# A graph network on one core: a batch's message sums share one PSUM bank and one stored block

## The chip, the cores and the metric

The kernel runs on one core of a Trainium2 chip. The metric is the device time in microseconds (us) of one execution, the lower the better. The profile times every instruction of one execution; its rows name the engines PE (TensorE's matmuls), PEld (its weight loads), DVE (VectorE), ACT (ScalarE), POOL (GpSimd) and SP (SyncE, which here only issues transfers). A name that ends in q, as SPq or PEldq, is the engine's sequencer: register work, semaphore waits and the issue of transfers.

## The reference

50000 nodes with 128 features, 50000 edges (src, dst), sorted by dst. Two parts follow each other; the change is in the two layers of the second.

```
x = layernorm(x + graph_convolution(x, src, dst))
h = x @ W_enc.T + b_enc
for l in range(2):
    m = concatenate([h[src], h[dst]], axis=-1)
    m = relu(m @ msg_W1[l].T + msg_b1[l])
    m = m @ msg_W2[l].T + msg_b2[l]
    agg = segment_sum(m, dst)
    upd = concatenate([h, agg], axis=-1) @ upd_W[l].T + upd_b[l]
    h = layer_norm(h + upd)
out = layernorm(x + h @ W_out.T + b_out)
```

## The kernel before

The work is a row of stages with a barrier of all engines behind each: rank, place and plan (they sort the edges into tiles and make tables), edges, conv and nodes (the convolution), and then for each layer `edges0`/`edges1` (message stage: `edge_stage` with `degrees` false) and `nodes0`/`nodes1` (node stage: `node_stage`). The second node stage also makes the output ("final").

**Tiles and steps.** Edges are cut into 392 tiles of 128, nodes into 392 tiles of 128, four to a chunk of 512 nodes, 98 chunks. A list of 784 steps walks through both: step s belongs to one edge tile and one node tile, and advances either one. Four steps make a batch, so a message stage has 196 batches. As dst is denser at low numbers and the walk starts at the high ones, a batch of the first 49 takes 1.4 new edge tiles on the mean and one of the last 49 takes 2.9.

**A batch in the message stage.** GpSimd gathers the src rows of each edge tile from `table_p` with an indirect transfer into `ring` (64 tiles; L851), in groups of four, 392 gathers in all; before it reuses a place it waits for the batch that read it last (`tile_end`, `s_pq`). SyncE loads the dst side, `q_ring`, chunk by chunk. ScalarE makes a one-hot matrix `turned` (L965, L967). PE's `combine` adds, for each of the four steps, the gathered rows (a product with the identity, L1011) and the dst rows picked by `turned` (L1012) in `ps_m`. ScalarE takes the relu into `msg` (L979). PE's `segment` multiplies it with `onehot`, which VectorE makes in `hot` (L868), into four column blocks of `ps_a` (L1021), one for each step. PE's order is: segment of batch i-2, combine of batch i. VectorE's `chain` then adds each step's block into its node tile in `acc` (L883), a sum that is kept in SBUF for 8 chunks; each of the four waits for the one ahead (`s_chain`). A chunk that is complete is stored by SyncE as one block of `table_t` (L826), 98 stores for a layer, and the next `q_ring` chunk is then loaded (L828).

**The node stage.** For chunk c SyncE's `load` brings the sums (`in_a` from `table_t`, L1250) and the layer's input (`in_z`, L1256), each 256 KB; PE's `update` (L1381, L1382), `flip_z` and `project` take 20 matmuls for a chunk; `store` of chunk c-7 puts `table_z` and `table_p` away (L1269, L1271). In the final stage SyncE brings `in_z` of the first layer again (L1261) and stores the output of chunk c-11 (L1266). The order on SyncE is fixed, in a hardware loop over four chunks at a time:

```
pipelined(sp, [(load, 0)] + ([(load_x1, 4), (store, 11)] if final else [(store, 7)]))
```

`load` waits until PE has used the buffer of chunk c-4 (`s_sum`). The four input buffers let the loads run up to three chunks ahead.

Of the kernel before, what the change touches and what calls it, by code (L numbers as in the profile page):

```python
# [8 lines left out]
P = 128  # L9
N, E, D, L = 50000, 50000, 128, 2  # L10
J = 4
# [19 lines left out]
HR, QR, BEHIND = 3, 3, 2  # L31
XR = 4
# [51 lines left out]
def parts(c):  # L84

    return LAST if is_last(c) else P

# [428 lines left out]
def plan_stage(nc, m):  # L516

    K = TP // 4
    with ExitStack() as ctx:
# [16 lines left out]
        n_s, n_c, e_s, lo, hi, loc, ge, past, within = (sb(n, [P, S]) for n in ("n_s", "n_c", "e_s", "lo", "hi", "loc", "ge", "past", "within"))  # L536
        ti = sb("ti", [1, 9, S], I32)
        tf, ends = sb("tf", [1, 3, NCHUNK]), sb("ends", [1, 4, 3 * EW], I32)
# [10 lines left out]
        with nc.Block() as block:  # L549
# [20 lines left out]
            def _(dve):  # L570
# [53 lines left out]
                nc.vector.memset(ends[:], 1)  # L624
                link(nc.vector.tensor_copy(int_row[:, 0, :], m.incl[:, 0:TP]))
# [4 lines left out]
                dve.sem_inc(s_rows, 1)  # L630

# [31 lines left out]
                link(nc.vector.tensor_scalar(ge[:], lo[:], m.lane[:], None, ALU.is_le))  # L663
                link(nc.vector.tensor_tensor(within[:], ge[:], past[:], ALU.mult))
# [25 lines left out]
                pack(table[:, :, 1], 5, [of(8, 3)] + [of(3, j) for j in range(4)], 7)  # L690
                nc.vector.tensor_copy(m.slots[:, 0:NB], table[:, :, 1])
# [9 lines left out]
                for k, to in ((0, m.chunk_end), (3, m.tile_end)):  # L701
                    pack(to[:, 0:EW], 10, [ends[:, k, :].rearrange("o (w j) -> o w j", j=3)[:, :, j] for j in range(3)], 10)
# [61 lines left out]
def edge_stage(nc, m, table, table_q, agg, degrees, x=None):  # L764


    F = P + 1 if degrees else P
    AW = W if degrees else P
    AR = 3 if degrees else QR
    where = (lambda j: (j // 2) * 512 + (j % 2) * W) if degrees else (lambda j: j * P)  # L770
    with ExitStack() as ctx:
# [3 lines left out]
        ring, first = m.ring, PRE // 4 if degrees else 0  # L775
        q_ring = None if degrees else sb("q_ring", [P, RC * CH])
        acc = sb("acc", [P, 4 * RC * AW])
        onehot = sb("onehot", [P, HR, 4, P])
        if not degrees:
            turned, msg = sb("turned", [P, QR, CH]), sb("msg", [P, QR, CH])  # L780
            d_ring = sb("d_ring", [P, DR, DB * CH], F16)
            ps_m = pb("ps_m", 512, QR)
        else:
            xin, x_t, r_out = sb("xin", [P, XR, CH]), sb("x_t", [P, 2, CH]), sb("r_out", [P, XR, CH])
# [13 lines left out]
        with nc.Block() as block:  # L798
# [35 lines left out]
            def _(pool):  # L834
                if degrees:
                    pool.sem_inc(s_prow, first)
# [717 lines left out]
```

## Time and profile before

| | us |
|---|---|
| device time, median of 3 runs (3956.29 to 3964.6) | 3957.3 |
| the profiled execution: its span, first to last instruction | 3444.6 |
| median less that span (what lies around it) | 512.7 |
| message stage of layer 0, from its first gather to the next stage's first load | 544.5 |
| node stage of layer 0, from its first load to the next stage's first gather | 410.4 |
| final node stage, from its first load to the end of the span | 367.5 |

The page of the profile gives no own device time for the profiled execution beside its span. The span is made of stages one after another, so the sum of the stages' lengths is the span; whatever is saved or lost in a stage is saved or lost in the time, and what lies around the span stays.

### The profile page before, as it was taken

To read this page: it belongs to the slowest core of one execution; us is meant where nothing else is said; L and a number is where in the kernel's file an instruction comes from. 1 tells how busy PE (TensorE), PEld (TensorE's weight loads), DVE (VectorE), ACT (ScalarE), POOL (GpSimd) and SP (SyncE) were. 2 spreads that over 40 slices of the span, in tenths; PEclk is the share of its full clock that TensorE was granted. 3 is DMA by queue.
4 is the path that set the end of the run, shared out by engine and by line. 5 is a ranking of instruction groups with operands and counts; after the bars stand their busy time and mean duration, and the time that the engine had idled before them with its cause. 6 is when DMAs were issued, how large, how long until landed. Compare 5 with 4: busy or idle time off the path is not lost. (4 is left out here: it accounts for less than half of the span.)

```text
span 3444.6 us, 92529 instructions
## 1 busy us (share of the span) xinstructions
PE 2975.2 (86%) x25312; PEld 2674.1 (78%) x25312; DVE 2700.0 (78%) x8634; ACT 2379.7 (69%) x5642; POOL 1846.0 (54%) x1782
## 2 busy tenths in 40 slices
PE   4975656777767789997999998999979999989998
PEld 3753334555543378987999998999979999989998
DVE  9999967888856688885777776666657777769998
ACT  3779945777742368886777775666657777759999
POOL 0000036577755533335776776555547767766664
PEclk9999988999979989999999999999989999999999
DMA  0027635777649989997776654999977766548887
GB/s 21 2 69 229 223 103 162 221 219 215 195 139 340 346 280 355 366 356 250 225 221 208 191 158 123 327 327 326 328 239 229 221 210 194 164 129 287 296 295 240
DMA packets 460711, 777.79 MB, mean 226 GB/s; under 512 B 113689, under 2 KB 115865, under 8 KB 460393
## 3 DMA queue, kind: packets, MB, share of 16 engines
q1 hardware_dynamic: 355046, 548.85, 48.2%
q10 hardware_dynamic: 67714, 147.73, 12.5%
q0 software_dynamic: 37632, 77.15, 9.2%
q8 instruction: 178, 2.92, 0.3%
q14 instruction: 141, 1.15, 0.1%
HBM read 451.50 MB, written 321.78 MB: 224 GB/s over the span
## 5 line engine op out<-in xcount | busy, mean ns | idle before, releaser
L883 DVE SCALAR_TENSOR_TENSOR edges_acc<-edges_acc,keep,edges_ps_a 128x128 f32 (+1 forms) x2352 | 820.3, 349 | 272.1 <-issue 145.9
L851 POOL DMA_INDIRECT ring<-table_p,esrc x784 | 787.5, 1004 | 313.3 <-issue 206.0
L1011 PE MATMUL edges_ps_m<-ring,ident 128*128 x3136 | 609.7, 276 | 33.8 <-POOLq L840 33.8
L1012 PE MATMUL edges_ps_m<-edges_q_ring,edges_turned 128*128 x3136 | 608.8, 276 | 0.0
L1011 PEld LDWEIGHTS edges_ps_m<-ring,ident 128*128 128x128 f32 x3136 | 478.6, 193 | 34.7 <-ACT edges_turned L967 17.7
L1012 PEld LDWEIGHTS edges_ps_m<-edges_q_ring,edges_turned 128*128 128x128 f32 x3136 | 478.8, 193 | 0.0
L979 ACT ACTIVATE edges_msg<-edges_ps_m 128x512 f32<-128x512 f32 x392 | 234.2, 597 | 295.5 <-PE edges_ps_m L1012 294.7
L1021 PE MATMUL edges_ps_a<-edges_onehot,edges_msg 128*128 128x128 f32 x3136 | 414.0, 275 | 0.0
L851 POOL DMA_INDIRECT ring<-table_h,esrc x344 | 327.7, 953 | 138.5 <-issue 93.5
L1021 PEld LDWEIGHTS edges_ps_a<-edges_onehot,edges_msg 128*128 128x128 f32 x3136 | 381.7, 192 | 0.0
L868 DVE TENSOR_TENSOR edges_onehot<-iota,drel 128x512 f32<-128x512 f16 x441 | 305.0, 692 | 96.1 <-PE edges_ps_a L1021 94.0
L1286 POOL TENSOR_TENSOR nodes_extra<-ub,deg 128x512 f32<-128x512 f32 x196 | 203.8, 1040 | 285.8 <-DVE nodes_y L1443 244.9
L1036 PEld LDWEIGHTS edges_ps_a<-ring,edges_onehot 128*128 128x128 f32 x1568 | 195.5, 196 | 175.9 <-issue 104.1
L1381 PE MATMUL nodes_ps_y<-uw,nodes_in_a 128*128 128x128 f32 x1568 | 306.0, 277 | 19.4 <-DMA nodes_in_z<-table_z 19.4
L1382 PE MATMUL nodes_ps_y<-wproj,nodes_in_z 128*128 128x128 f32 x1568 | 305.5, 277 | 0.0
L1407 PE MATMUL nodes_ps_p<-wproj,nodes_z_t 128*128 128x128 f32 x1568 | 303.2, 275 | 0.0
L1406 PE MATMUL nodes_ps_q<-wproj,nodes_z_t 128*128 128x128 f32 x1568 | 303.1, 275 | 0.0
L1036 PE MATMUL edges_ps_a<-ring,edges_onehot 128*128 x1568 | 224.0, 287 | 90.8 <-DVE edges_acc L883 47.5
L965 ACT ACTIVATE edges_turned<-edges_d_ring,minus_lane 128x512 f32<-128x512 f16 x392 | 279.3, 712 | 21.8 <-DMA edges_d_ring<-table_d 21.6
L967 ACT ACTIVATE edges_turned<-edges_turned,one 128x512 f32<-128x512 f32 x392 | 283.1, 722 | 12.8
L1454 DVE BATCH_NORM_STATS2 nodes_st<-nodes_y 128x6 f32<-128x128 f32 x1176 | 255.6, 280 | 6.9
L1289 POOL TENSOR_TENSOR nodes_extra<-nodes_extra,bu 128x512 f32<-128x512 f32 x196 | 249.8, 1274 | 15.4
(315 smaller groups left out, 6776.2 us busy)
## 6 DMA issues: line engine op xcount, KB each, us to landing
table_z<-nodes_z_t SPq DMA_DIRECT2D x196, 256.0 KB, 5.0
table_p<-nodes_p_out SPq DMA_DIRECT2D x196, 256.0 KB
table_q<-nodes_q_out ACTq DMA_DIRECT2D x196, 256.0 KB
edges_q_ring<-table_q SPq DMA_DIRECT2D x196, 256.0 KB, 4.8
edges_d_ring<-table_d ACTq DMA_DIRECT2D x98, 512.0 KB
table_t<-edges_acc SPq DMA_DIRECT2D x196, 256.0 KB
nodes_in_a<-table_t SPq DMA_DIRECT2D x196, 256.0 KB
nodes_in_z<-table_z SPq DMA_DIRECT2D x196, 256.0 KB, 4.3
```

The costliest lines, as they stand in the source:

```text
L851: nc.gpsimd.indirect_dma_start(out=ring[:, e % RE * W:e % RE * W + P], out_offset=None, in_=table[:, :], in_offset=bass.IndirectOffsetOnAx ...
L868: nc.vector.tensor_tensor(onehot[:, i % HR, :, :], m.iota[:, 0:P].unsqueeze(1).to_broadcast([P, 4, P]), m.drel[:, 4 * i:4 * i + 4].unsquee ...
L883: nc.vector.scalar_tensor_tensor(out=to, in0=to, scalar=m.keep[:, s:s + 1], in1=ps_a[:, i % AR, where(j):where(j) + F], op0=ALU.mult, op1= ...
L967: nc.scalar.activation(to, to, ACT.Relu, bias=m.one[:], scale=-1.0).then_inc(s_turned, 1)
L1011: nc.tensor.matmul(to, m.ident[:], rows[j], start=True, stop=False)
L1012: last = nc.tensor.matmul(to, turned[:, i % QR, j * P:(j + 1) * P], slots[j], start=False, stop=True)
L1021: last = nc.tensor.matmul(ps_a[:, i % QR, j * P:(j + 1) * P], msg[:, i % QR, j * P:(j + 1) * P], onehot[:, i % HR, j, :], start=True, stop ...
L1036: last = nc.tensor.matmul(ps_a[:, i % AR, where(j):where(j) + F], onehot[:, i % HR, j, :], rows[j], start=True, stop=True)
L1381: nc.tensor.matmul(to, part(in_a, b, j), m.uw[:, layer, :], start=True, stop=False)
L1382: last = nc.tensor.matmul(to, part(in_z, b, j), m.wproj[:, layer, 2 * D:3 * D], start=False, stop=True)
L1406: nc.tensor.matmul(part(ps_q, b % 2, j), part(z_t, b, j), m.wproj[:, nxt, D:2 * D], start=True, stop=True)
L1407: last = nc.tensor.matmul(part(ps_p, b % 2, j), part(z_t, b, j), m.wproj[:, nxt, 0:D], start=True, stop=True)
```

## The change

**Message stage** (now `message_stage`; `edge_stage` keeps only the convolution). `combine` leaves the identity product out for steps 0 and 1 of a batch (`ADDED = 2`); VectorE's `add_rows` adds those two gathered rows to `ps_m` where it lies in PSUM. `segment` puts the four products of a batch into one PSUM bank at the place of the node tile, counted from the tile of step 0 (`m.wins` holds the distances), so that steps of one tile add up in PSUM. VectorE's `move` then takes the bank to SBUF, `window`: the first 128 columns with what the window before carried over for that tile, the other 384 by a copy. ScalarE stores every window as one block of `table_w` (`store`), 196 for a layer and 256 KB each. `q_ring` chunks wait for `combine` (`q_end`) and no longer for a finished sum.

**Node stage.** The sums of a node tile now lie in some block of `table_w`; `m.where` says in which one and at which of its four places. `load` reads four words of it and brings the four tiles of a chunk with four transfers of 64 KB.

**Plan stage.** It makes the tables `wins`, `carry`, `where` and `q_end`.

The diff, cut to its core:

```diff
+ADDED, WR, STORE = 2, 6, 4
...
-                def chain(i):
-                    dve.wait_ge(s_seg, i + 1)
-                    for j in range(4):
-                        s = 4 * i + j
-                        if s >= 1:
-                            dve.wait_ge(s_chain, s)
-                        nc.vector.scalar_tensor_tensor(out=to, in0=to, scalar=m.keep[:, s:s + 1], in1=ps_a[:, i % AR, where(j):where(j) + F],
-                                                       op0=ALU.mult, op1=ALU.add).then_inc(s_chain, 1)
+                def add_rows(i):
+                    rows = [ring[:, bass.ds(value(i, 1 + j), P)] for j in range(ADDED)]
+                    dve.wait_ge(s_pq, i + 1)
+                    for j in range(ADDED):
+                        last = nc.vector.tensor_tensor(tile(ps_m, i, j), tile(ps_m, i, j), rows[j], ALU.add)
+                    last.then_inc(s_add, 1)
+
+                def move(i):
+                    carried = window[:, (i - 1) % WR, bass.ds(value(i, 0) % J * P, P)]
+                    dve.wait_ge(s_seg, i + 1)
+                    if i >= 1:
+                        dve.wait_ge(s_win, 2 * i)
+                    if i >= WR:
+                        dve.wait_ge(s_out[i % WR], 16 * (i // WR))
+                    nc.vector.scalar_tensor_tensor(out=window[:, i % WR, 0:P], in0=carried, scalar=m.keep[:, 4 * i:4 * i + 1], in1=tile(ps_a, i, 0),
+                                                   op0=ALU.mult, op1=ALU.add).then_inc(s_win, 1)
+                    nc.vector.tensor_copy(window[:, i % WR, P:CH], ps_a[:, i % QR, P:CH]).then_inc(s_win, 1)
+
+                for i in range(NB + BEHIND):
+                    if i >= BEHIND:
+                        move(i - BEHIND)
+                    if i + 1 < NB:
+                        fetch(i + 1)
+                        hot(i + 1)
+                    if i < NB:
+                        add_rows(i)
...
+                def store(i):
+                    act.wait_ge(s_win, 2 * i + 2)
+                    act.dma_start(m.table_w[i * P:(i + 1) * P, :], window[:, i % WR, :]).then_inc(s_out[i % WR], 16)
...
                     for i in range(NB):
                         if i + 2 < NB:
                             turn(i + 2)
-                        act.wait_ge(s_pq, i + 1)
+                    if i >= STORE:
+                        store(i - STORE)
+                    act.wait_ge(s_add, i + 1)
...
-                    for j in range(4):
-                        nc.tensor.matmul(to, m.ident[:], rows[j], start=True, stop=False)
-                        last = nc.tensor.matmul(to, turned[:, i % QR, j * P:(j + 1) * P], slots[j], start=False, stop=True)
+                    for j in range(J):
+                        if j >= ADDED:
+                            nc.tensor.matmul(tile(ps_m, i, j), m.ident[:], rows[j], start=True, stop=False)
+                        last = nc.tensor.matmul(tile(ps_m, i, j), tile(turned, i, j), slots[j], start=j < ADDED, stop=True)
...
+                    if i % 4 == 0:
+                        spots[0] = loaded(nc, mybir.EngineType.PE, m.wins[0:1, i:i + 4])
+                    to = [tile(ps_a, i, 0)] + [ps_a[:, i % QR, bass.ds(spots[0][i % 4] // (1 << (2 * j - 2)) % J * P, P)] for j in range(1, J)]
+                    for j in range(J):
+                        last = nc.tensor.matmul(to[j], tile(msg, i, j), onehot[:, i % HR, j, :], start=j == 0, stop=True, skip_group_check=True)
...
                     else:
                         sp.dma_start(in_z[:, b, :], m.table_z[layer][bass.ds(c * P, P), :]).then_inc(s_z[b], 16)
+                        at = loaded(nc, mybir.EngineType.SP, m.where[0:1, bass.ds((NC - 1) * J - c * J, J)], S - 1)
+                        for j in range(J):
+                            sp.dma_start(in_a[:, b, j * P:(j + 1) * P],
+                                         m.table_w[bass.ds(at[j] // J * P, P), bass.ds(at[j] % J * P, P)]).then_inc(s_a[b], 16)
```

**SyncE in the node stage.** These are all of SyncE's instructions for one chunk inside the hardware loop of the layer 0 node stage, before the change; ISA is a group of register operations that sets an address.

```order
L1248 REGISTER_ALU
L1250 ISA
L1250 DMA nodes_in_a<-table_t 128x512
L1256 DMA nodes_in_z<-table_z 128x512
L1268 REGISTER_ALU
L1269 ISA
L1269 DMA table_z<-nodes_z_t 128x512
L1271 ISA
L1271 DMA table_p<-nodes_p_out 128x512
```

This is how the same chunk begins in the changed kernel; L92 is the helper that reads words of a table into registers.

```order
L1387 REGISTER_ALU
L1395 ISA
L1395 DMA nodes_in_z<-table_z 128x512
L92 REGISTER_ALU
L92 ISA
L92 TENSOR_LOAD where
L1398 ISA
L1398 REGISTER_ALU
L1398 DMA nodes_in_a<-table_w 128x128
```

The last three rows stand there four times; after them come the rows of `table_z` and `table_p` as before. A chunk's transfers on this queue go from four to seven, and a read of registers stands between the first and the second.

**PE in the message stage.** One batch before the change (segment of one batch, combine of another), where the names are those of the section on the kernel.

```order
L1021 MATMUL edges_ps_a<-edges_onehot,edges_msg 128x128 x4
L990 REGISTER_ALU x2
L1000 ISA x7
L1011 MATMUL edges_ps_m<-ring,ident 128x128
L1012 MATMUL edges_ps_m<-edges_q_ring,edges_turned 128x128
```

The last two rows stand there four times. After the change:

```order
L1193 ISA x3
L1201 MATMUL edges_ps_a<-edges_onehot,edges_msg 128x128 x4
L1174 REGISTER_ALU x2
L1178 ISA x5
L1185 MATMUL edges_ps_m<-edges_q_ring,edges_turned 128x128 x2
L1184 MATMUL edges_ps_m<-ring,ident 128x128
```

One more L1185, L1184 and L1185 follow. The matmuls of a batch go from 12 to 10 and the address groups from 7 to 8, three of which now stand ahead of the segment.

**VectorE in the message stage** had `hot`, four L876 ISA and four L883 for a batch. It now has this.

```order
L1103 ISA
L1109 SCALAR_TENSOR_TENSOR edges_window<-edges_window,keep,edges_ps_a 128x128
L1111 COPY edges_window<-edges_ps_a 128x384
L92 TENSOR_LOAD carry
L1089 TENSOR_TENSOR edges_onehot<-iota,drel 128x512
L1095 ISA
L1098 TENSOR_TENSOR edges_ps_m<-edges_ps_m,ring 128x128 x2
```

Three of four chained sums are gone; a copy of 384 columns, two additions and, every second batch, a read of registers have come.

## Rows read from the trace of the kernel before

**Rows 1.** The first line of any view.

```profile
core 0 of [0], span 3444.6 us
```

**Rows 2.** Windows by stage: stretch, length, busy time of PE, PEld, DVE, ACT, POOL, PEclk, DMA share.

```profile
228.00:468.00 240.00, 139.62 (x784) 73.86 (x784) 213.44 (x545) 229.56 (x785) 0.31 (x1) 0.97 0.67 215
...
980.00:1000.00 20.00, 11.12 (x44) 7.46 (x44) 8.66 (x22) 7.24 (x18) 15.12 (x17) 0.67 0.30 82
1577.00:2118.00 541.00, 527.79 (x4704) 527.52 (x4704) 407.51 (x979) 378.27 (x588) 394.09 (x392) 0.99 0.63 191
2118.00:2532.00 414.00, 396.99 (x3528) 396.02 (x3528) 257.73 (x1081) 248.63 (x686) 226.59 (x196) 0.98 0.92 311
...
3077.00:3444.00 367.00, 350.92 (x3136) 349.67 (x3136) 344.72 (x1960) 331.50 (x1078) 226.37 (x196) 0.98 0.86 280
```

**Rows 3.** Groups of instructions by line: count | busy us, mean ns | idle before, releasers.

```profile
L851 POOL DMA_INDIRECT ring<-table_p,esrc x784 | 787.5, 1004 | 313.3 <-issue 206.0 <-POOLq L1527 52.3 <-PE edges_ps_m L1012 43.7
...
L883 DVE SCALAR_TENSOR_TENSOR edges_acc<-edges_acc,keep,edges_ps_a 128x128 f32 x1568 | 545.5, 348 | 170.0 <-issue 124.6 <-DVE edges_acc L883 3.0 <-PE edges_ps_a L1021 0.6
```

**Rows 4.** Timeline of the gathers: the stage's first and last.

```profile
1577.42 0.99 POOL L851 DMA_INDIRECT ring<-table_p,esrc  x1 [21.00 <-POOLq L1527]
...
2100.38 0.94 POOL L851 DMA_INDIRECT ring<-table_p,esrc  x1 [0.30 <-issue]
```

**Rows 5.** Sequencers, two lines of code: durations in ns, minimum, median, maximum.

```profile
L1000 PEldq FUSED_REGOPS  x3332: 62/176/200, 544.6 to 3066.9; - x196
...
L794 PEldq TENSOR_LOAD <-steps x294: 327/332/1162, 543.8 to 3061.8; - x147
...
L794 SPq TENSOR_LOAD <-chunk_end x15: 523/815/1220, 543.8 to 3031.7; - x15
```

**Rows 6.** Groups of VectorE in the plan stage.

```profile
L595 DVE COPY wproj<-plan_ps_c 128x384 f32<-128x384 f32 x1 | 0.6, 558 | 6.5 <-PE plan_ps_s L718 6.5
...
L604 DVE TENSOR_TENSOR bu<-plan_ps_s,rows 128x128 f32<-128x128 f32 x2 | 0.6, 280 | 0.0
```

**Rows 7.** Timeline of SyncE, layer 0 node stage: start, length, transfer.

```profile
2300.79 0.35 SPq L1250 DMA_DIRECT2D nodes_in_a<-table_t  x1
2301.24 0.41 SPq L1256 DMA_DIRECT2D nodes_in_z<-table_z  x1
2301.84 0.35 SPq L1269 DMA_DIRECT2D table_z<-nodes_z_t  x1
2304.22 0.35 SPq L1271 DMA_DIRECT2D table_p<-nodes_p_out  x1
```

**Rows 8.** Timeline of SyncE, final node stage.

```profile
3252.39 0.33 SPq L1261 DMA_DIRECT2D nodes_in_x<-table_z  x1
3253.02 0.36 SPq L1266 DMA_DIRECT2D out<-nodes_res  x1
```

**Rows 9.** Waits of SyncE, 2150 to 2500 and 3100 to 3420: total, times, longest.

```profile
SPq L1271 <- DVE nodes_p_out L1484: 148.2, 87, 2.2
...
SPq L1261 <- PE nodes_ps_q L1404: 113.8, 90, 2.7
```

**Rows 10.** SyncE's address groups of line 1250, 2150 to 2500, in ns.

```profile
L1250 SPq FUSED_REGOPS  x84: 46/60/60, 2160.1 to 2493.1; - x84
```

**Rows 11.** Timeline of SyncE: first and last sum load of both node stages.

```profile
2121.93 0.34 SPq L1250 DMA_DIRECT2D nodes_in_a<-table_t  x1
...
2500.94 0.46 SPq L1250 DMA_DIRECT2D nodes_in_a<-table_t  x1
...
3077.08 0.34 SPq L1250 DMA_DIRECT2D nodes_in_a<-table_t  x1
...
3409.43 0.43 SPq L1250 DMA_DIRECT2D nodes_in_a<-table_t  x1
```

**Rows 12.** The page's queues: packets, MB, share of 16 engines' span.

```profile
q1 hardware_dynamic: 355046, 548.85, 48.2%
...
q0 software_dynamic: 37632, 77.15, 9.2%
```

More of the change, by code:

```diff
@@ L86, in parts, with loaded @@
     return LAST if is_last(c) else P
+def loaded(nc, engine, at, most=2 ** 31 - 1):
+    return nc.values_load_multi_w_load_instructions(
+        at, engines=(engine,), min_val=0, max_val=most, skip_runtime_bounds_check_because="the table is made in range")[1]
 def slot_uses(ring, b):
@@ L891, in relu_x @@
                     nc.vector.tensor_scalar(to, ps_r[:, 0, :], 0.0, None, ALU.max).then_inc(s_r, 1)
-                lag = 2 if degrees else BEHIND + 1
-                for i in range(NB + (lag + 2 if degrees else lag)):
-                    if i < NB and (not degrees or i % SHARE == SHARE - 1):
+                lag = 2
+                for i in range(NB + lag + 2):
+                    if i < NB and i % SHARE == SHARE - 1:
                         hot(i)
@@ new lines, in _ @@
+                for c in range(XR):
+                    load_x(c)
+                for i in range(2 * NC + 7):
+                    if i < NB and i % SHARE != SHARE - 1:
+                        hot_a(i)
+                    if i % 2 == 1:
+                        if 0 <= (i - 3) // 2 < NC:
+                            copy_x((i - 3) // 2)
+                        if XR <= (i + 3) // 2 < NC:
+                            load_x((i + 3) // 2)
+                    elif i >= 8 and (i - 8) // 2 % RING != HELD:
+                        keep((i - 8) // 2)
@@ L981, in _ @@
+                for b in range(XR):
+                    if b != HELD:
+                        act.wait_ge(s_kept[b], 16 * slot_uses(XR, b))
+                act.wait_ge(s_root, 1)
+                nc.scalar.activation(m.norm[:, 1, :], m.norm[:, 1, :], ACT.Sqrt).then_inc(s_root, 1)
             @block.tensor
@@ L1015, in segment @@
-                def segment(i):
-                    pe.wait_ge(s_hot_v, i + 1)
-                    pe.wait_ge(s_msg, i + 1)
-                    if i >= QR:
-                        pe.wait_ge(s_chain, 4 * (i - QR + 1))
-                    for j in range(4):
-                        last = nc.tensor.matmul(ps_a[:, i % QR, j * P:(j + 1) * P], msg[:, i % QR, j * P:(j + 1) * P], onehot[:, i % HR, j, :], start=True, stop=True)
-                    last.then_inc(s_seg, 1)
-                def sum_rows(i):
-                    fetch(i)
-                    landed, rows = due(i), addressed([row(i, j) for j in range(4)])
+                    due = [nc.tensor.compute_val(word[0][i % 2 * 2 + k] & 127) for k in range(2)]
@@ L1027, in sum_rows @@
+                    rows = [ring[:, bass.ds(word[0][i % 2 * 2] // (1 << (7 + 6 * j)) % 64 * W, F)] for j in range(4)]
+                    for at in rows:
+                        nc.tensor.lower_ap(at)
                     if i % SHARE == SHARE - 1:
@@ L1067, in batch @@
                         combine(i)
-                for i in range(NB + 2):
-                    batch(i)
 def held(m, turn):
```

388 lines of the change are left out of this document (232 added, 156 removed).

## Prediction

> **What bounds the kernel now.** I first read the windows by stage [rows 2]. The message stage (1577 to 2118) has PE busy for 527.79 of 541 us; the node stage behind it (2118 to 2532) 396.99 of 414; the final one 350.92 of 367. So PE looks like the bound in all stages that the change touches, and 12 matmuls of a batch cost 527.79 / 196 = 2.69 us, 0.224 each. That is the figure that makes the change look good: ten matmuls would be 2.24 us.
>
> The second view is that of the gathers, and there the reader is to see that another engine is nearly as late. A gather takes 1004 ns on the mean [rows 3] and the next one starts 0.30 us behind its end even when it waits for nothing [rows 4], so 392 of them need 392 x 1.304 = 511 us. From the start of the first to the end of the last 2101.32 - 1577.42 = 523.9 us went by [rows 4]. GpSimd was thus held up for only 13 us in a stage of 541.
>
> The third is SyncE's timeline in the node stages. It is never counted busy, but it is an engine with an order of its own. In the layer 0 node stage four transfers go out per chunk: 2300.79, 2301.24, 2301.84, then nothing until 2304.22 [rows 7]. Two with only a register move between them are 0.45 us apart, with an address group between them 0.60. The hole is a wait for VectorE's `p_out`: 148.2 us in 87 waits, 1.70 us a chunk; in the final stage it waits 113.8 us in 90 times for PE, 1.26 us a chunk [rows 9]. The chunk's own pace is (2500.94 - 2121.93) / 97 = 3.91 us in the first and (3409.43 - 3077.08) / 97 = 3.43 us in the final stage [rows 11]. SyncE has 1.3 to 1.7 us of slack a chunk and no more.
>
> **The change, part by part.**
>
> *Message stage, PE and VectorE.* PE goes to 10 x 0.224 = 2.24 us a batch. VectorE is busy 407.51 / 196 = 2.08 us now [rows 2]; three sums of 348 ns [rows 3] go, a copy of 384 columns, 558 ns, and two additions of 280 ns come [rows 6] (the same shapes, PSUM as a source; the additions also write PSUM, which no row shows; as long as the sum of 348 ns they would be 0.14 us dearer): 2.08 - 1.04 + 0.56 + 0.56 = 2.16 us, up to 2.3. PE's sequencer makes 8 address groups of 176 ns instead of 7 and reads words three times in four batches, not two, at 332 ns [rows 5]: 1.41 + 0.25 = 1.7 us besides its waits. ScalarE's new store is issued behind an activation that is still running. So a batch could be done in some 2.3 to 2.6 us.
>
> *Message stage, gathers.* They are untouched: 511 us. A batch at 2.6 us would fill that (some 10 us until the first one, then 196 x 2.6 = 510), so all that PE gains below 2.6 us is waiting for rows, above all in the last quarter, where a batch needs 2.9 tiles and thus 3.8 us of gathers. From the last gather's end to the next stage's first load it is 2121.93 - 2101.32 = 20.6 us now [rows 4, 11]; PE will then have little left, which I take as 17. The stage becomes 511 + 17 = 528 instead of 544.5: 16 us less, and **33 us less** for both layers. Bounds: 0, if a batch takes 2.69 for other reasons; 40, if PE is so close behind that the tail halves. The doubled stores (25 MB more at a DMA share of 0.63 [rows 2]) lie beside this.
>
> *Node stages, DMA.* Each sum load becomes four with runs of 512 bytes. The nearest rows for such runs are the gathers': queue q0 takes 9.2% for 77.15 MB, q1 48.2% for 548.85 [rows 12], which is 1.36 times as much for a byte. One fifth of the layer 0 node stage's traffic (two loads and three stores of 256 KB) would cost that, so the DMA share of 0.92 goes to 0.99: just hidden, 0 to 10 us by itself.
>
> *Node stages, SyncE.* This is the term that decides. For one chunk of the layer 0 node stage, in its order: the `in_z` load 0.60; the read of `where` with its address; four loads of `in_a`; the `table_z` store 0.66 (0.60 [rows 7] and a register operation, an estimate); the `table_p` store 0.60.
> - Read of four words: PE's takes 332 ns, SyncE's own, of eight words, 815 ns in the median [rows 5]. I take 0.45 and 0.16 for its index: 0.61. Bounds 0.5 and 1.0.
> - One `in_a` load: a transfer with an address group is 0.60 behind the next [rows 7], with groups of 46 to 60 ns [rows 10]. Here the group has a shift, a mask and two products, as PE's of 176 ns [rows 5] (0.12 more), and a register operation stands behind it. 0.76 each, 3.04 for four. Bounds 0.60 (SyncE does it as fast as its present ones) and 0.85.
>
> Sum: 0.60 + 0.61 + 3.04 + 0.66 + 0.60 = **5.5 us**, against a pace of 3.91. In the final stage `in_x` and the output, 0.63 apart [rows 8], take the places of the stores: **5.6 us** against 3.43. SyncE becomes the bound. Its waits vanish, the four input buffers run empty, and PE waits for `in_a`. Until the first stores are due the queue has less to do. Layer 0: 7 chunks without two stores, 90 with: 7 x 4.3 + 90 x 5.5 = 525 us from first to last load, now 379.0, so **+146**. Final: 4 x 4.3 + 7 x 4.95 + 86 x 5.6 = 534, now 332.4, so **+201**. Some 14 of 98 chunks lie outside the loop and have fixed addresses for the plain transfers: about -12 for both.
>
> All bounds cheap: 4.7 and 4.8 us a chunk, which gives 447 and 456 us, +68 and +124. All dear: 6.3 and 6.4 us, 602 and 610 us, +223 and +278.
>
> By the Trainium skill (DMA: Bandwidth & Descriptors, Latency and other measured facts) a `tensor_load` has a floor of about 600 ns. PE's four-word loads of 332 ns [rows 5] contradict it as a floor, SyncE's of 523 and more do not. By that rule the read would be 0.15 us dearer and the result 29 us later, an estimate; the sum goes by the rows.
>
> *Plan stage.* Some twenty more operations on one partition in VectorE's chain, none longer than the 558 ns of [rows 6]: 0 to 11 us, taken as 5.
>
> Sum: -33 + 146 + 201 - 12 + 5 = +307 on the profiled span of 3444.6 [rows 1], to 3752. What lies around the span, 512.7 us to the median of 3957.3, stays: 3957.3 + 307 = **4264, said as 4260 us**.
>
> **The rivals.**
>
> *A, SyncE binds both node stages and the message stages gain little* (0.80). For it: the count of seven transfers, each at least 0.45 behind the other, is 3.2 us before any address or read; with the cheapest address work it is already above 3.91 and 3.43. Cheap it is 3957 + 68 + 124 - 40 - 12 = about 4100, dear 3957 + 223 + 278 + 11 - 33 - 12 = about 4420.
>
> *B, SyncE stays hidden, faster* (0.07). This is the other side: if a transfer of 64 KB needed only some 0.3 us on the queue and its address work ran beside the issue before it, the three more and the read would cost 1.3 to 1.7 us, the present slack [rows 9]. It decides at 3.91 and 3.43 us a chunk. Then only the message stages and the plan count: 3957 - 33 + 5 = 3929. Against it: the issues are 0.33 to 0.41 us long whatever they carry, and none overlaps the next [rows 7, 8].
>
> *C, the message stages get slower too* (0.10). The way from `combine` to `segment` now goes over VectorE (`s_add`) as well, and PE's sequencer stands at `segment`'s wait with five address groups of the next combine behind it. Were a batch to take 2.9 us, each message stage would end 0.3 x 196 = 59 us later than in A: 4260 + 118 = 4380. It decides at 2.6 us. Against it: `segment` follows its combine by more than a batch, and the addition and relu take about 1.2 us of that.
>
> *D, the DMA engines bind the node stages.* The skill says under Bandwidth on the same page that transfers should be at least 1 MiB, and that those under 64 KB are dominated by descriptors; 64 KB is given 0.95 us of DMA time. As a mechanism here: if four loads took 1.36 times their bytes' time and more, a chunk at the share of 0.92 [rows 2] would rise past its pace. At twice the time for a byte one fifth more work gives 0.92 x 1.2 = 1.1, 0.1 x 410 = 41 us for layer 0, and the final stage with 0.86 next to nothing: 3929 + 41 = 3970 if SyncE were hidden, nothing if it is not (0.02).
>
> PE's clock could make A dearer. It had fallen between 980 and 1000, with PE busy 56% of the time, but the place stage kept 0.97 at 58% [rows 2]; at 3.5 / 5.6 = 62% in the final stage I expect it to hold.
>
> **How the numbers follow.** The time is that of A. The range reaches from just under A cheap to A dear, 4090 to 4420; it holds most of A and C. About 0.2% (8 us) is what a measurement of this kernel can tell from no change. Faster: B, 0.07. Same: D and accidents between, 0.02. Slower: 0.91.
>
> **What would show it.** In the changed profile SyncE issues without holes in the node stages, at 5.5 and 5.6 us a chunk, and its waits of 148.2 and 113.8 us are gone. PE waits at `update` for `in_a`. The DMA share there falls to about 0.7. In the message stages the gathers run from end to end in some 511 us and PE waits for them in the last quarter. I am wrong if seven transfers fit into less than 4 us, and off in size if the read of `where` or the address groups are not 0.61 and 0.76 us a piece.

## The result, and the profile after

| | us |
|---|---|
| before, median of its runs in this comparison (3956.29 to 3966.79) | 3960.95 |
| changed kernel, median of its four runs (4396.93 to 4417.14, and 7439.92) | 4414.35 |
| ratio, with its 95% interval | 1.1129 (1.1098 to 1.1159) |
| profiled execution of the changed kernel: time, span | 4411.57, 4409.9 |

The changed kernel is 11.3% slower. One of its four executions, at 7439.92 us, was disturbed: the ratio is that of the other three, whose median is 4411.57. Its profile also says something about the first profile of before: here hardly 2 us lie around the span, not 512.7. So before was profiled once more, as the first experiment (e1_before_again, below): span 3963.1, time 3964.82. The execution of [rows 1] ran its message stages and the convolution's edges stage much faster than the timed executions do, and nothing like 512 us lies around a span: in e1_before_again the two message stages are 182 and 178 us longer, and 160 us of the difference lie ahead of them. From here on, the stages of after stand beside those of this second profile.

The stages by windows, e1_before_again first: two message stages, then two node stages, in the columns of [rows 2].

```profile
1737.00:2463.00 726.00, 587.51 (x4704) 565.63 (x4704) 402.07 (x981) 373.33 (x588) 381.32 (x392) 0.90 0.46 143
...
2872.00:3595.00 723.00, 582.04 (x4704) 560.15 (x4704) 402.36 (x981) 372.37 (x588) 379.54 (x392) 0.91 0.46 144
...
2463.00:2872.00 409.00, 396.89 (x3528) 395.92 (x3528) 256.73 (x1078) 248.54 (x686) 226.47 (x196) 0.98 0.93 314
3595.00:3963.00 368.00, 351.15 (x3136) 349.90 (x3136) 344.71 (x1960) 331.41 (x1078) 226.31 (x196) 0.98 0.86 279
```

The same four of the changed kernel.

```profile
1745.00:2502.00 757.00, 528.68 (x3920) 502.26 (x3920) 366.85 (x984) 375.49 (x588) 392.79 (x393) 0.87 0.54 171
...
3090.00:3844.00 754.00, 524.48 (x3920) 498.76 (x3920) 366.85 (x984) 375.50 (x588) 396.33 (x393) 0.86 0.54 172
...
2502.00:3090.00 588.00, 455.69 (x3528) 437.38 (x3528) 258.72 (x1079) 256.46 (x686) 225.35 (x196) 0.92 0.68 219
3844.00:4409.00 565.00, 408.50 (x3136) 387.21 (x3136) 357.25 (x1960) 332.74 (x1078) 225.11 (x196) 0.93 0.61 182
```

To a tenth, with a node stage taken from its first sum load: message stages 726.1 and 723.1, now 756.8 and 754.1 (+31 each); layer 0 node stage 409.3, now 587.8 (+179); final 367.5, now 565.5 (+198). That is 438 of the 447 us between the spans; the other 9 are a later start of the first message stage, which varies by as much between runs. The node stages of the first profile (410.4 and 367.5) are confirmed; its message stages (544.5) are not. PE's idle share is the thing to compare: in the first profile 16 of 544 us, here 138 of 726, and 228 of 757 after the change.

What SyncE does in the layer 0 node stage now, from its timeline (answers to [rows 7]).

```profile
2802.20 0.35 SPq L1395 DMA_DIRECT2D nodes_in_z<-table_z  x1
2804.03 2.62 SPq L1398 DMA_DIRECT2D nodes_in_a<-table_w  x4
2806.94 0.35 SPq L1412 DMA_DIRECT2D table_z<-nodes_z_t  x1
2807.49 0.36 SPq L1414 DMA_DIRECT2D table_p<-nodes_p_out  x1
2808.11 0.35 SPq L1395 DMA_DIRECT2D nodes_in_z<-table_z  x1
```

One chunk is 5.91 us here, and from each transfer to the next the queue only issues, computes places and reads the table. SyncE's waits from 2502 to 3090, and in the second piece PE's of the same stage and of the final one (answers to [rows 9]):

```profile
SPq L1414 <- DVE nodes_p_out L1627: 7.7, 7, 2.3
```

```profile
PE nodes_ps_y L1524 <- DMA nodes_in_a<-table_w: 129.1, 72, 10.6
...
PE nodes_ps_y L1524 <- DMA nodes_in_a<-table_w: 148.4, 87, 9.7
```

SyncE waited 148.2 us for `p_out` in most of this stage before [rows 9]; now 7.7 in all of it. In the final stage its 113.8 us of waiting for PE are 3.1 now, with 15.3 for the output. The wait has moved to PE, which stands at `update` until the sums land. The bound has changed from PE to SyncE's queue.

The read of `where` on SyncE (ns: min/median/max) in the layer 0 node stage and then in the final one; in the second piece the address group and the issue of a sum load, both stages together:

```profile
L92 SPq TENSOR_LOAD <-where x97: 298/673/1262, 2506.6 to 3064.0; - x97
...
L92 SPq TENSOR_LOAD <-where x97: 296/396/887, 3847.5 to 4378.7; - x97
```

```profile
L1398 SPq FUSED_REGOPS  x784: 205/213/258, 2502.0 to 4381.9; - x196
...
L1398 SPq DMA_DIRECT2D nodes_in_a<-table_w x784: 332/333/978, 2502.5 to 4382.3; - x196
```

### The profile page after: what moved, and what is told of

It reads as the page before. It is cut to its first block and busy times, and to the rows that moved or that the text cites. A ratio compares the mean times of both kernels' runs of the same rounds, so it can differ in the third digit from the quotient of the medians.

```text
span 4409.9 us, 92906 instructions
## 1 busy us (share of the span) xinstructions
PE 3132.4 (71%) x23744; PEld 2737.7 (62%) x23744; DVE 2636.6 (60%) x8665; ACT 2382.9 (54%) x5642; POOL 1847.2 (42%) x1782
## 5 line engine op out<-in xcount | busy, mean ns | idle before, releaser
L1185 PE MATMUL edges_ps_m<-edges_q_ring,edges_turned 128*128 x3136 | 604.1, 297 | 137.6 <-issue 84.3
L1201 PE MATMUL edges_ps_a<-edges_onehot,edges_msg 128*128 128x128 f32 x3136 | 467.1, 297 | 304.9 <-issue 284.1
L1201 PEld LDWEIGHTS edges_ps_a<-edges_onehot,edges_msg 128*128 128x128 f32 x3136 | 423.3, 210 | 331.6 <-issue 331.1
L1185 PEld LDWEIGHTS edges_ps_m<-edges_q_ring,edges_turned 128*128 128x128 f32 x3136 | 485.8, 208 | 164.4 <-issue 129.6
L1524 PE MATMUL nodes_ps_y<-uw,nodes_in_a 128*128 128x128 f32 x1568 | 350.7, 309 | 278.4 <-DMA nodes_in_a<-table_w 277.5
L1524 PEld LDWEIGHTS nodes_ps_y<-uw,nodes_in_a 128*128 128x128 f32 x1568 | 265.3, 212 | 316.5 <-issue 210.0
L1098 DVE TENSOR_TENSOR edges_ps_m<-edges_ps_m,ring 128x128 f32<-128x128 f32 x784 | 194.5, 294 | 426.7 <-DMA table_z<-nodes_z_t 236.3
L892 DVE SCALAR_TENSOR_TENSOR edges_acc<-edges_acc,keep,edges_ps_a 128x129 f32 x784 | 274.8, 350 | 222.3 <-remote 108.2
L1586 DVE TENSOR_TENSOR nodes_y<-nodes_ps_y,nodes_extra 128x512 f32<-128x512 f32 x196 | 135.5, 691 | 434.6 <-PE nodes_ps_y L1525 359.7
L1184 PE MATMUL edges_ps_m<-ring,ident 128*128 x1568 | 326.4, 291 | 17.5 <-issue 17.5
L1109 DVE SCALAR_TENSOR_TENSOR edges_window<-edges_window,keep,edges_ps_a 128x128 f32<-128x128 f32 x392 | 135.5, 346 | 330.4 <-PE edges_ps_a L1201 196.0
L936 ACT ACTIVATE edges_onehot<-iota,minus_drel 128x128 f32<-128x128 f16 x588 | 188.5, 392 | 218.5 <-remote 103.3
```

Of the source, the lines that this page charges most:

```text
L892: nc.vector.scalar_tensor_tensor(out=to, in0=to, scalar=m.keep[:, s:s + 1], in1=ps_a[:, i % AR, where(j):where(j) + F], op0=ALU.mult, op1= ...
L1184: nc.tensor.matmul(tile(ps_m, i, j), m.ident[:], rows[j], start=True, stop=False)
L1185: last = nc.tensor.matmul(tile(ps_m, i, j), tile(turned, i, j), slots[j], start=j < ADDED, stop=True)
L1201: last = nc.tensor.matmul(to[j], tile(msg, i, j), onehot[:, i % HR, j, :], start=j == 0, stop=True, skip_group_check=True)
L1524: nc.tensor.matmul(to, part(in_a, b, j), m.uw[:, layer, :], start=True, stop=False)
```

## The experiments

In the experiments called one_load, four_fixed, added0 and the later ones built on them, the node stages load blocks that do not hold the chunk's sums; bytes and work are the same. The diffs are shortened: semaphore increments and lines that only follow from the ones shown are left out. "Stage" below is the length of a message stage from its first gather to the next stage's first sum load, layer 0 and layer 1. The time of before was 3961.13, 3967.18 and 3959.41 in the three groups in which kernels shared a chip, and 4001.1 for the last kernel.

### Before, profiled again

> The kernel before, unchanged, profiled once more. The changed kernel's profiled span is 4409.9 us with a time of 4411.57, so hardly anything lies around it, while 512.7 us seemed to lie around the span of before. Theory 'other conditions': the first profile of before came from an execution whose clock was higher (0.97) than that of the timed ones; a new one gives a span within 3 us of its time, near 3957, with TensorE's clock near 0.90 and the convolution's edges stage at some 620 us as in the changed kernel, not 479. Rival 'around': span again 3445 and 512 around it; then the changed kernel's stages really are 965 us longer and something in it makes even the untouched convolution slower.

Span 3963.1, time 3964.82, clock 0.925. The theory 'other conditions' holds (the clock is a little higher than it said); what the condition was is not known. The two profiles of one kernel differ in the stages with gathers alone. The difference is not spread evenly. Windows of 60 us within the first 80 us of the message stage, of e1_before_again and then of the first profile:

```profile
1760.00:1820.00 60.00, 7.68 (x23) 5.86 (x23) 2.08 (x5) 1.93 (x3) 43.82 (x46) 0.50 0.21 60
```

```profile
1600.00:1660.00 60.00, 60.00 (x540) 60.00 (x539) 46.04 (x111) 43.35 (x68) 46.28 (x46) 1.00 0.74 227
```

GpSimd does the same in both (46 gathers); PE is busy for 60 of 60 us in one and 7.68 in the other. What PE does in such a stretch (timeline, e1_before_again), and when it ends; below it GpSimd's last gathers before it:

```profile
1801.74 0.37 PE L1012 MATMUL edges_ps_m<-edges_q_ring,edges_turned 128*128 x1 [2.43 <-issue]
1803.84 0.37 PE L1012 MATMUL edges_ps_m<-edges_q_ring,edges_turned 128*128 x1 [1.73 <-issue]
1807.34 0.37 PE L1011 MATMUL edges_ps_m<-ring,ident 128*128 x1 [3.12 <-issue]
...
1829.61 0.76 PE L1011 MATMUL edges_ps_m<-ring,ident 128*128 x2
1830.16 0.63 PE L1012 MATMUL edges_ps_m<-edges_q_ring,edges_turned 128*128 x2
1830.59 0.52 PE L1011 MATMUL edges_ps_m<-ring,ident 128*128 x2
```

```profile
1815.47 0.94 POOL L851 DMA_INDIRECT ring<-table_p,esrc  x1 [0.30 <-issue]
1816.72 0.95 POOL L851 DMA_INDIRECT ring<-table_p,esrc  x1 [0.30 <-issue]
```

Inside one batch's combine, with no semaphore to wait for ("issue"), PE's products start 1.4 to 3.5 us apart, most of them 2 us and more. The last of 64 gathers that GpSimd makes without a pause (the ring is full then) ends at 1817.7; from 1827 on PE is at its usual pace. By the starts of the relus the first 20 batches take 125.1 us (first profile: 53.0), the next 80 some 59 for each 20, the last full 20 before the end 85.3. I call this a hold-up; shorter ones occur in the rest of the stage, and one of them is shown further down.

Code that is loaded late would look alike. This is the queue of instructions in the window 1760 to 1820 of e1_before_again (packets, MB, share of 16 engines' span).

```profile
q8 instruction: 1, 0.02, 0.1%
```

Its one packet took 0.94 us, and the median of this queue's 178 packets is 0.96. A slow transfer of code is thus not seen; whether PE got instructions late for another reason, the trace does not show.

### What each part of the change costs

```diff
 # e2_one_load: node stage
-at = loaded(nc, ..SP, m.where[0:1, ...], S - 1)
-for j in range(J):
-    sp.dma_start(in_a[:, b, j * P:(j + 1) * P], m.table_w[bass.ds(at[j] // J * P, P), bass.ds(at[j] % J * P, P)])
+sp.dma_start(in_a[:, b, :], m.table_w[bass.ds(c * P, P), :])
 # e3_four_fixed: four loads, neither the read nor computed places
+for j in range(J):
+    sp.dma_start(in_a[:, b, j * P:(j + 1) * P], m.table_w[bass.ds(c * P, P), j * P:(j + 1) * P])
 # e4_added0: e2_one_load and
-ADDED = 2
+ADDED = 0     # s_add becomes s_pq for ScalarE and GpSimd
```

> The changed kernel with the sum load of the node stages put back to one transfer of 256 KB at c * P (the block read is then not the one that holds the chunk's sums, so the node stage computes with other data of the same size). Theory 'SyncE': the four small loads and the read of where are the whole loss in the node stages, so each of them goes back to its length of before; the time falls by 310 to 450 us, to 3965 to 4100, and what is left over the time of before is the message stages. Rival 'message': the message stages carry most of the loss, and this kernel keeps more than 250 of the 453 us, above 4200.

> The changed kernel with four sum loads of 64 KB per chunk, but at c * P and fixed columns and without the read of where (other data of the same size, as in e2_one_load). Theory 'count of issues': three more issues at 0.45 to 0.60 us each put 1.5 us on SyncE's chunk, to 4.6 to 4.8 us, above 3.9 and 3.4: 40 to 60% of the node stages' loss stays, 130 to 230 us above e2_one_load. Rival 'address work': the issues fit into SyncE's slack and only the read and the four computed addresses cost; then this is within 40 us of e2_one_load.

> e2_one_load with ADDED = 0: VectorE adds no rows, PE makes 12 matmuls for a batch again, ScalarE and GpSimd wait for PE; the one bank and the window stay. Theory 'VectorE link': in the changed kernel the addition stands behind move and hot on VectorE, and relu, segment, move wait for it in turn, so without it the message stages become shorter by 0.3 us a batch or more, 60 us each, 120 in all less than e2_one_load. Rival 'PE matmuls': two matmuls more are 0.45 us a batch, 88 us a stage, 176 more in all than e2_one_load.

| | time | ratio to before | stages | node stages |
|---|---|---|---|---|
| changed kernel | 4414.35 | 1.1129 | 756.8, 754.1 | 587.8, 565.5 |
| e3_four_fixed | 4085.38 | 1.0317 (1.0297 to 1.0338) | 753.2, 744.4 | 418.5, 403.2 |
| e2_one_load | 4041.63 | 1.0210 (1.0187 to 1.0234) | 759.6, 756.6 | 409.7, 367.2 |
| e4_added0 | 3999.88 | 1.0110 (1.0084 to 1.0136) | 738.4, 737.0 | 408.7, 367.9 |

The read of `where` and the computed places cost 329 us, three more transfers a chunk 44, VectorE's additions 42 (net of the two matmuls that they save), and bank, window and plan 39. SyncE carries 373 of 453, as the theory 'SyncE' of e2_one_load said. In the profiles 26 of the last 39 us lie in the message stages; which part of the new segment and window costs them was not tried. Of e3_four_fixed's rivals "address work" is nearer: 44 us against a bound of 40, and 130 to 230 for the other. But the count of issues is seen too: seven transfers with fixed columns take 3.86 us a chunk in the final stage, where 3.43 was the pace, and the stage is 36 us longer; in layer 0 they take 4.06 and it is 9 longer. e4_added0 falsifies "PE matmuls": with 12 matmuls the message stages are shorter by 20 us each than with 10. That is the sign of 'VectorE link', and a third of its size (60 us each).

### Without gathers

```diff
 # GpSimd, message stages (before; and e2_one_load)
+pool.sem_inc(s_prow, NCHUNK)
+return
```

> The kernel before without the 784 gathers of the two message stages (GpSimd reports all rows as landed at once; PE reads what the convolution left in the ring, so the sums are of other rows). In the new profile of before a message stage is 726 us, in its first 80 us GpSimd gathers without a pause, and PE's instructions stand 0.7 to 1.4 us apart from 1758 to 1827 although they wait for nothing. Theory 'gathers hold PE up': without them that stretch and all waits for rows are gone, a message stage is 196 x 2.69 + 20 = 547 us as in the first profile of before, and the time 3961 - 2 x 179 = about 3600. Rival 'something at the start of the stage' (the code of the stage, which isn't a loop, or the loads of q_ring and the table for turned): the first 20 batches still take some 125 us, a message stage 615, the time about 3740.

> e2_one_load without the gathers of the message stages, as in e5_before_no_gathers. It shows what a batch of the changed message stage costs when no row is late. Theory 'PE bound' (the prediction): 10 matmuls instead of 12, 2.3 to 2.6 us a batch, a message stage of 475 to 535 us and so 15 to 70 us shorter than that of e5_before_no_gathers; then the additions only hurt by what they do to the gathers (a place in the ring comes free later, behind VectorE). Rival 'link': the round over VectorE (combine, add_rows, relu, segment, move) is the pace, 2.9 us or more a batch, 590 us or more, longer than e5_before_no_gathers.

3602.04 (ratio 0.9081, 0.9057 to 0.9104) and 3539.96 (0.8933, 0.8907 to 0.8959). Windows of the middle of the message stage, e5 and then e6:

```profile
1800.00:2200.00 400.00, 400.00 (x3585) 400.00 (x3583) 307.88 (x748) 288.18 (x449) 0.00 (x0) 1.00 0.49 157
```

```profile
1800.00:2200.00 400.00, 376.28 (x3193) 363.38 (x3192) 300.19 (x799) 307.74 (x479) 0.00 (x0) 1.00 0.63 210
```

By the starts of the relus a batch takes 2.70 us before and 2.53 us after the change. Both theories hold: the gathers, not the start of the stage, hold PE up; and the changed message stage really is shorter, by 31 us (half the difference of the times), as long as nothing holds PE up; by the profiles, from the first relu to the next stage's first sum load, it is 36 and 35 us. With gathers it is longer by 31.

### GpSimd's lead

```diff
 # e7_short_ring, kernel before, message stages (the ring has 16 groups)
-if g >= RE // 4: k = g - RE // 4
+if g >= 6:       k = g - 6
 # e9_growing_lead
+ahead = min(RE // 4, 5 + g // 5)     # k = g - ahead
```

> The kernel before with GpSimd at most 24 tiles (six groups) ahead of PE in the message stages instead of 64. Theory 'a run of gathers without a pause holds PE up': the free run at the start is 24 gathers, 30 us, and not 64, 80 us; PE's 70 lost us shrink to some 25, GpSimd never gets so far ahead that it must stand still for 45 us, and the stage, which ends with the gathers, becomes 50 to 100 us shorter: 3961 - 100 to 200 = 3760 to 3860. Rival 'lead': the lead of 64 tiles is what carries the stage through its last quarter (2.9 tiles a batch); with 24 the stage ends up to 40 x 1.3 = 52 us later, 3961 + 104 = 4065.

> The kernel before with GpSimd's lead over PE growing in the message stages: 5 groups of four tiles at the start, one more after every fifth group, at most 16 (the ring). e7_short_ring (6 groups throughout) took 72 instead of 125 us for its first 20 batches, but 157 instead of 126 for its last 36. Theory 'run and lead': both hold, a short free run at the start keeps the 53 us gained there, and the full lead in the last quarter the 29 us that e7_short_ring lost, 2 x 29 = 58 us below e7_short_ring, 3856; at least 3880 to 3840. Rival 'the lead must be paid': whenever GpSimd gains a group on PE it gathers without a pause and holds PE up as at the start, so what the growth costs is what it brings: same as e7_short_ring, 3914.

e7_short_ring: 3913.96, ratio 0.9887 (0.9839 to 0.9934), stages 699.8 and 702.6. The first 20 batches take 71.9 instead of 125.1 us, the last 35 take 156.8 instead of 125.6. The theory is right in kind, but of its gain of 100 to 200 us only 53 came: the rival's loss is in it too. e9_growing_lead: 3968.26, ratio 1.0024 (1.0011 to 1.0036). Its first 20 batches take 78.8 us, but the next 80 take 277 instead of 237; the last 35 take 124.1, as before (125.6). The rival is right in kind: what GpSimd gains on PE is paid with hold-ups, here with 54 us more than the rival's 3914.

### Why the shorter batch is slower where there are gathers

A hold-up in e2_one_load, from the timelines of PE, VectorE and ScalarE.

```profile
2018.55 0.39 PE L1185 MATMUL edges_ps_m<-edges_q_ring,edges_turned 128*128 x2
2022.52 1.74 PE L1201 MATMUL edges_ps_a<-edges_onehot,edges_msg 128*128 128x128 f32 x7 [3.58 <-issue]
```

```profile
2021.29 0.50 DVE L1098 TENSOR_TENSOR edges_ps_m<-edges_ps_m,ring 128x128 f32<-128x128 f32 x2 [2.90 <-DMA table_z<-nodes_z_t]
```

```profile
2021.82 0.60 ACT L1160 ACTIVATE edges_msg<-edges_ps_m 128x512 f32<-128x512 f32 x1 [5.18 <-issue]
```

Combine is recorded as ending at 2018.94 (PE's ends are modelled), but the addition, which waits for nothing else, starts at 2021.29, so combine really ended some 2.3 us later: the trace has a semaphore event at 2021.27, 0.02 us ahead of the addition, as it has ahead of most additions. The DMA that the profile names as what the addition waited for can't be it: the program has no such wait there. From 2021.29 the chain runs addition, relu, segment, and PE, whose order is segment i-2 and then combine i, has nothing else to do until 2022.52.

```diff
 # e11_late_release: e4_added0, GpSimd frees the ring on the relu
-pool.wait_ge(s_pq, third(ends, k))
+pool.wait_ge(s_msg, third(ends, k))
 # e12_deeper: e2_one_load, message stage only
+HR, QR, BEHIND = 4, 4, 3        # 3, 3, 2
```

> e4_added0 (no additions on VectorE) with GpSimd waiting for the relu of the batch that read a place of the ring (s_msg) and not for its products (s_pq), so that places come free a microsecond or more later, later than behind the additions of e2_one_load. Theory 'late release' (the additions make the message stages 20 us longer because the ring comes free later): 20 us or more a stage, 4000 + 40 = 4040 or more. Rival 'longer round' (PE stands at segment, because combine, add_rows, relu, segment is longer by the addition whenever PE was held up): no change from e4_added0, 4000.

> e2_one_load with one batch more between combine and segment in the message stages (BEHIND 3 instead of 2, four buffers instead of three for turned, msg, onehot, ps_m and ps_a). Theory 'longer round': PE no longer stands at segment after each hold-up (331 and 284 us idle in front of the segment's weight loads and products in the changed kernel), the message stages get back at least the 20 us each that the additions cost and some 10 of the 62 us that they save where no gathers run: 4042 - 60 = 3980, or down to 3960. Rival 'late release': nothing changes for GpSimd, 4042.

e11_late_release: 4056.86, ratio 1.0258 (1.0227 to 1.0289), stages 758.9 and 763.8, 20 and 27 us longer than e4_added0. e12_deeper: 3965.32, ratio 0.9999 (0.9982 to 1.0017), stages 726.1 and 724.7, 33 and 32 us shorter than e2_one_load. PE's idle time in front of the segment and GpSimd's wait for a place in the ring, layer 0 message stage, in e4_added0, e2_one_load, e11_late_release and e12_deeper:

```profile
POOL ring L1063 <- PE edges_ps_m L1183: 162.4, 56, 11.0
...
PE edges_ps_a L1199 <- issue: 32.5, 10, 20.6
```

```profile
POOL ring L1063 <- DVE edges_ps_m L1098: 203.7, 56, 12.0
PE edges_ps_a L1201 <- issue: 138.3, 49, 32.4
```

```profile
POOL ring L1063 <- ACT edges_msg L1158: 207.6, 66, 12.9
...
PE edges_ps_a L1199 <- issue: 35.5, 16, 20.6
```

```profile
POOL ring L1064 <- DVE edges_ps_m L1099: 152.5, 35, 12.1
...
PE edges_ps_a L1202 <- issue: 49.5, 62, 3.1
```

The additions do two things. They lengthen the round from combine to segment, so PE stands in front of the segment for 138 us instead of 33; and a place in the ring comes free later. Each alone is seen to matter: a late release costs 20 to 27 us without touching PE's idle time there (e11), and one batch more between combine and segment brings back 32 us with the release left as it is (e12). Neither theory excludes the other, and e12 does not part them fully: with PE less late, GpSimd's wait for a place fell too, from 203.7 to 152.5 us. How the 20 us of the additions divide between them stays open, since e11's release is later than that of the additions by an amount that the runs don't fix.

### Two queues

```diff
 # e8_two_queues, node stages: SyncE's loop over j ends at 2; ScalarE, first in its order for a chunk:
+act.wait_ge(s_sum, c - (RING - 1))
+at = loaded(nc, ..Activation, m.where[0:1, bass.ds((NC - 1) * J - c * J + 2, 2)], S - 1)
+for j in range(2):
+    act.dma_start(in_a[:, b, (2 + j) * P:(3 + j) * P], m.table_w[...])
```

> The changed kernel with ScalarE's queue issuing the loads of tiles 2 and 3 of a chunk in the node stages (its own read of two words of where, two computed addresses), SyncE those of tiles 0 and 1. The bytes, their number and their pieces are the same. Theory 'SyncE's queue binds': SyncE's chunk goes from 5.83 and 5.55 to 4.3 and 4.0 us, 97 x 1.5 = 147 us less in each node stage, if ScalarE (2.5 us busy a chunk in the layer 0 stage, 3.4 in the final one) can issue beside its activations: 4414 - 295 = 4120; if it can't in the final stage, 4414 - 147 = 4267 or more. Rival 'DMA binds' (four pieces of 64 KB with runs of 512 bytes): no change, 4414.

4255.95, ratio 1.0714 (1.0673 to 1.0756); 158 us less than the changed kernel, so not the DMA engines but the queue binds. But a chunk takes 4.90 and 4.91 us, not 4.3 and 4.0. ScalarE's timeline:

```profile
2703.24 1.09 ACTq L1495 DMA_DIRECT2D nodes_in_a<-table_w  x2
2704.54 0.30 ACT L1451 ACTIVATE nodes_rstd<-nodes_mv,eps 128x4 f32<-128x4 f32 x1 [3.79 <-issue]
```

ScalarE's activations stand still for 3.79 us here, while its queue stores `table_q`, reads `where` and issues two loads. In the layer 0 stage there are 54 such stops of up to 3.8 us, 125.9 us in all; in the final stage 72 of up to 2.4, 121.9 us. The read of two words is a large part (ns, minimum, median, maximum, layer 0 stage).

```profile
L92 ACTq TENSOR_LOAD <-where x97: 487/907/1692, 2512.4 to 2984.8; - x97
```

The expectation that it could issue beside its activations failed. ScalarE became the bound in both stages: PE waits for its `z` (66 and 71 us), SyncE again for the stores' data (95 and 94 us).

### The version that beats both

e7_short_ring with e12's order as well (`HR, QR, BEHIND = (3, 3, 2) if degrees else (4, 4, 3)`, and PE's loop to `NB + BEHIND`).

> The kernel before with both edits that shortened a message stage: GpSimd at most 24 tiles ahead (e7_short_ring, 3914) and three batches instead of two between combine and segment with four buffers (as in e12_deeper, there 77 us less). Theory 'the round matters only where it is long': before the change PE stands at segment for 104 and 90 us in both message stages, a third of what it does in the changed kernel (331 and 284), of which a deeper order can give back some 40; 3914 - 40 = 3874. Rival 'hold-ups of PE alone': without VectorE in the round two batches are enough, and PE's time is lost in combine itself; same as e7_short_ring, 3914.

3932.16 where before takes 4001.1: ratio 0.9816 (0.9797 to 0.9835). It stands better beside before than e7_short_ring does (0.9887), but in another comparison, in which before takes 4001.1 and not 3967.18. Its message stages are as long as there (699.2 and 702.6 against 699.8 and 702.6), and the 16 us by which its profiled span is longer than that of e7_short_ring (3928.7, 3912.9) lie ahead of the first of them. So the profile supports the rival: the short lead is what helps, and without VectorE in the round two batches are enough. Why before takes 34 us longer in this comparison is not explained, and neither are the few tenths of a per cent between the two ratios.

## Why the prediction was right, and where it was not

**SyncE becomes the bound of both node stages.** Right, with its signs: no holes on SyncE, its waits gone (148.2 to 7.7 us), PE waiting for `in_a`, a DMA share of 0.68 and 0.61 (said: 0.7), 5.83 and 5.55 us a chunk from first to last load (said: 525 and 534 us for 97 of them, 5.4 and 5.5 on the mean). The node stages grew by 179 and 198 (said: 146 and 201, less 12 for both).

**The terms of that sum.** From one `in_a` load to the next 0.767 us on the mean (said 0.76), from the last of the four to the next transfer 0.59 and 0.60; the step from `in_z` to the first `in_a` 1.73 us in layer 0 and 1.42 in the final stage, where 0.60 + 0.61 were put. The read of `where` is the term that was mis-sized: with its address work 1.13 and 0.82 us, the load of registers alone 673 and 396 ns in the median, where 0.45 was taken. Part of it is a matter of where a term is booked: the address group of the first `in_a` load lies in this step, and the last `in_a` is cheaper by it. For the whole chunk the mean steps add up to 5.97 us in layer 0 (said 5.5) and to 5.63 in the final stage (said 5.6). By the Trainium skill (DMA: Bandwidth & Descriptors, Latency and other measured facts) such a load has a floor of about 600 ns. The layer 0 median is above it and the final stage's is not, with a minimum of 296, so as a floor it falls. As a price 600 ns was nearer than my 450 in layer 0 (673), and farther in the final stage (396). The prediction also read SyncE's loads of 523 ns and more [rows 5] as no contradiction to a floor of 600; they are one.

**DMA (0 to 10 us, rival D).** Right: e3_four_fixed's layer 0 stage is 9 us longer at a DMA share of 0.95, and e8_two_queues became faster with the same pieces.

**Rival B (SyncE hidden).** Wrong by two steps: even with fixed columns a transfer takes some 0.55 us on the queue, not 0.3, so that seven need 3.86; and the read and the computed places add 1.7 to 1.8.

**The message stages (-33 us).** Wrong in sign: +62. The step that failed is "They are untouched: 511 us", with the one it stood on, that GpSimd was held up for 13 us. In a timed execution the gathers of a stage go from 1737.1 to 2410.2, 673 us, GpSimd waits 159 of them for PE, and PE is held up by the gathers; in the changed kernel they take 706.5. The batch itself was sized rightly (2.3 to 2.6; 2.53 without gathers, and 10 matmuls save 31 us a stage), and so was VectorE's work (an addition 294 ns, said 280; the copy 551, said 558). The tail of 17 us behind the last gather is 50.

**Rival C** named the mechanism in part, the way from combine to segment over VectorE, and dismissed it because "the addition and relu take about 1.2 us" of a slack of more than a batch. Without gathers that is so. With hold-ups of 2 us and more the slack is used up. Its price of 59 us a stage was too high: 31. What happened is A and C together. Of the 150 us between the sum of 4264 and the measured 4414, 95 are the message stages' (62 more instead of 33 less) and 42 the node stages' (377 instead of 335), so the time lies at the upper end of the range. That it lies inside all the same is owed to the range's width and not to the sum, which had the sign of the message stages wrong.

**What lies around the span (512.7 us).** Wrong, and it did no harm to the time only because it was added to both sides. That 512 us were missing was a sign that the profile showed an execution unlike the timed ones, and that its message stages could not be taken at their word.

**Clock.** In the final stage 0.93 against 0.98, so it held for the most part, as said. In the message stages it is 0.87 against 0.90, and 0.50 in the hold-up.

## What to carry to other kernels

Count the issues, address groups and register reads of a queue per loop turn, as if SyncE were a compute engine: here three more transfers, four computed places and one read of four words made a turn 1.9 to 2.1 us longer on an engine that never shows as busy, 377 us in all. Before a profile is used, set its span beside the timed median; where they differ by an eighth, profile again before any stage is priced. And a shorter batch can be worth nothing when its round gets longer, as here where products come late: judge it by how long PE can go on when its newest product comes late.

## What the runs showed of the hardware that was not expected

- PE's products stood 1.4 to 3.5 us apart, inside one batch and with nothing to wait for, while GpSimd made 64 gathers without a pause (PE busy 7.68 of 60 us, clock 0.50). Without gathers this was gone (PE busy 400 of 400 us). In one of two profiles of the same kernel it was absent with gathers too. What decides that, and by what resource the gathers reach PE, is open.
- The same load of four words took SyncE 673 ns in the median in one stage and 396 in another.
- The issue of transfers on ScalarE's queue, with a read of two words (907 ns in the median in the layer 0 stage, where SyncE's of four words took 433), kept its activations back for up to 3.8 us; it was no free second queue.
